# Last stage of a four-layer graph network: features in two 12-bit float32r pieces, adjacency in fp32 and bf16 pieces

## Time and profile before

| what | us |
|---|---|
| median of 3 runs | 3906.61 (3905.37 to 3919.26) |
| the profiled execution's own time | 3927.33 |
| its span, first to last instruction | 3925.3 |
| last stage in that span | 3150 to 3925.3 |
| PE busy over the span | 3393.5 (86%) |
| mean granted TensorE clock | 0.922 of 2.4 GHz |

### The profile page before, as it was taken

The page is one execution under the profiler, slowest core; times in us unless marked ns, Lnnn a source line. Parts: engine busy times, 40 slices in busy tenths (PEclk is TensorE's granted clock), DMA queues, the critical chain, the costliest instruction groups (busy, mean ns, idle before and its releaser), DMA issues. The chain is left out here.

```text
span 3925.3 us, 81257 instructions
## 1 busy us (share of the span) xinstructions
PE 3393.5 (86%) x22381; PEld 2072.9 (53%) x22381; DVE 1826.2 (47%) x5337; ACT 1453.8 (37%) x3467; POOL 1781.0 (45%) x1807
## 2 busy tenths in 40 slices
PE   4999999994875999999699989679888879999998
PEld 1566666662553555655355545345454535555554
DVE  4566666665854444453344444334444332353222
ACT  3555555552243454544233333223333331132122
POOL 1444444551015777774677777377777600000000
PEclk8988889996987999999889998789999989999999
DMA  3566666664836566665778787487777644543133
GB/s 116 170 186 192 187 184 185 178 177 80 255 116 176 157 183 176 184 178 133 201 208 223 217 229 200 118 228 208 203 205 207 164 151 171 177 153 109 55 116 123
DMA packets 717221, 675.09 MB, mean 172 GB/s; under 512 B 383123, under 2 KB 543738, under 8 KB 716810
## 3 DMA queue, kind: packets, MB, share of 16 engines
q1 hardware_dynamic: 623290, 466.05, 40.5%
q0 software_dynamic: 77008, 200.24, 18.9%
q10 hardware_dynamic: 16768, 6.91, 0.7%
HBM read 530.63 MB, written 142.28 MB: 171 GB/s over the span
## 5 line engine op out<-in xcount | busy, mean ns | idle before, releaser
L2190 POOL DMA_INDIRECT l_y<-s_lrows,l_src x1332 | 1331.9, 1000 | 456.7 <-issue 383.7
L3193 PE MATMUL ps<-nl_adj,nl_table 126*128 126x504 bf16 (+1 forms) x3150 | 631.2, 357 | 2.3 <-DVE nl_table L3428 2.3
L951 POOL DMA_INDIRECT em_gs<-s_rows,em_idx x400 | 389.6, 974 | 424.6 <-DMA em_idx<-in_sd 312.4
L3193 PEld LDWEIGHTS ps<-nl_adj,nl_table 126*128 126x128 bf16 x3150 | 301.8, 96 | 298.7 <-issue 5.0
L2230 PE MATMUL ps<-ident,l_y 128*128 128x128 f32 x1800 | 268.0, 285 | 205.7 <-DMA l_y<-s_lrows,l_src 124.1
L2273 PE MATMUL ps<-l_y,aw_pT 128*63 128x277 f32 x2700 | 384.8, 423 | 2.5 <-ACT aw_pT L2467 2.0
L2584 DVE TENSOR_TENSOR l_y<-l_y 128x768 f32<-128x768 f32 x225 | 214.0, 951 | 331.5 <-DMA l_y<-s_lrows,l_src 288.2
L2453 ACT ACTIVATE aw_yT<-ps 128x512 f32<-128x512 f32 (+1 forms) x525 | 262.0, 534 | 256.5 <-PE ps L2230 245.9
L2257 PE MATMUL ps<-aw_yT,aw_qt 128*63 128x384 f32 x1800 | 338.4, 499 | 6.9 <-DMA aw_yT<-s_dxT 6.9
L2230 PEld LDWEIGHTS ps<-ident,l_y 128*128 128x128 f32 x1800 | 205.2, 144 | 263.5 <-issue 201.8
L2619 DVE COPY aw_axd<-ps 128x252 f32<-128x252 f32 x225 | 94.6, 420 | 410.0 <-PE ps L2290 392.9
(11 more groups left out here) (375 smaller groups left out, 5872.9 us busy)
## 6 DMA issues: line engine op xcount, KB each, us to landing
nl_adj<-s_adj SPq DMA_DIRECT2D x20, 3100.8 KB
aw_yT<-s_dxT SPq DMA_DIRECT2D x150, 384.0 KB, 4.4
aw_geoS<-s_geoS SPq DMA_DIRECT2D x450, 94.5 KB
nl_adj<-s_adj SPq DMA_DIRECT2D x15, 2325.6 KB
ws_msg<-s_msg SPq DMA_DIRECT2D x75, 384.0 KB, 3.9
s_dxT<-aw_yT SPq DMA_DIRECT2D x75, 384.0 KB, 4.4
aw_qt<-s_qt SPq DMA_DIRECT2D x225, 126.0 KB
s_msg<-em_msg SPq DMA_DIRECT2D x100, 256.0 KB, 2.5
```

The source lines that it names most:

```text
L951: pool.indirect_dma_start(out=gs[:, u, j, :], out_offset=None, in_=d["rows0"], in_offset=bass.IndirectOffsetOnAxis(ap=idx[:, u, 2 * j:2 * ...
L2190: pool.indirect_dma_start(out=y[:, u, j, 0:W], out_offset=None, in_=table, in_offset=bass.IndirectOffsetOnAxis(ap=src[:, u, j:j + 1], axis ...
L3193: m = nc.tensor.matmul(k.ps[:, bank(i, p), 0:cols * WN], source[:, p, q, b, :], adj[:, a % 2, 0:cols, b * WN:(b + 1) * WN], start=b == 0 a ...
```

## The change

- The tables `table0` and `table1` hold the features as two pieces of type float32r. VectorE makes the first by clearing the low 12 bits of the fp32 word (`MASK`, a bitwise and), ScalarE copies it into the table (`HIGH`), and VectorE writes the difference as the second (`LO`). `REST` and `MID` go.
- `aggregate` has two matmuls for each source block and part, not three, both operands float32r. It goes over the adjacency in five pieces of five source blocks, both parts of `c2` within a piece.
- The adjacency stands in HBM in two banks: source blocks 0 to 14 in fp32, 15 to 24 in bf16, laid out by piece and partition. SyncE loads the three fp32 pieces of a turn straight into a ring of four buffers (`adj`). The two bf16 pieces go into a ring of three (`raw`), and POOL copies each into the ring of four, which widens it to float32r.
- `em` counts into the two banks with 315 and 210 columns (before: 273 and 273), ScalarE copies each bank for itself, and a window is stored with two DMAs.
- The positions of `make`, `turn` and `mix` in `aggregate` are other numbers, for the new order. The first adjacency load of the stage comes behind the loads of the weights, not ahead of them.
- VectorE waits, at the start of each turn, for its own last instruction of the turn before.

```diff
+PB = 5
+ADJ_BLOCKS = (15, 10)
+ADJ_TYPES = (F32, BF16)
+PIECES = tuple((bank, n) for bank in range(2) for n in range(ADJ_BLOCKS[bank] // PB))
+TOP12 = -4096
...
-                nc.scalar.activation(adj[:, v, :, h * HN:(h + 1) * HN].rearrange("p (q b) n -> p q b n", q=2),
-                                     k.ps[0:BM, ADJ:ADJ + 2, 0:KN].rearrange("p q (b n) -> p q b n", n=HN),
-                                     ACT.Copy).then_inc(adj_ok.sem, 1)
+                for q in range(2):
+                    nc.scalar.activation(adj[q][:, v, :, h * HN:(h + 1) * HN], k.ps[0:BM, ADJ + q, 0:KN[q]].rearrange("p (b n) -> p b n", n=HN),
+                                         ACT.Copy).then_inc(adj_ok.sem, 1)
...
-        table = [sb("table0", [BM, 1, 3, NB, D], BF16), sb("table1", [BM, 2, 3, NB, D], BF16)]
-        adj = sb("adj", [BM, 2, AW, NB * WN], BF16)
+        table = [sb("table0", [BM, 1, 2, NB, D], F32R), sb("table1", [BM, 2, 2, NB, D], F32R)]
+        RING, RAW = 4, 3
+        adj = sb("adj", [BM, RING, AW, PB * WN], F32R)
+        raw = sb("raw", [BM, RAW, AW, PB * WN], BF16)
...
+                for p, (bank, at) in enumerate(PIECES):
+                    g = NP_ * (i - AHEAD) + p
+                    piece = d[f"adj{bank}"][at, :, w:w + n, :]
+                    if DIRECT[p]:
+                        if g >= RING:
+                            sp.wait_ge(consumed, g - RING + 1)
+                        sp.dma_start(adj[:, g % RING, 0:n, :].bitcast(F32), piece).then_inc(adj_in[g % RING], 16)
+                    else:
+                        r = casts(g)
+                        if r >= RAW:
+                            sp.wait_ge(cast, r - RAW + 1)
+                        sp.dma_start(raw[:, r % RAW, 0:n, :], piece).then_inc(raw_in[r % RAW], 16)
...
         def _(pool):
-            nc.gpsimd.tensor_copy(idb[:, :], k.ident[:, :]).then_inc(made_id, 1)
+            nc.gpsimd.tensor_copy(idr[:, :], k.ident[0:BM, 0:BM]).then_inc(made_id, 1)
+            for i in range(AHEAD, len(turns)):
...
+                    r = casts(g)
+                    pool.wait_ge(raw_in[r % RAW], 16 * (r // RAW + 1))
+                    if g >= RING:
+                        pool.wait_ge(consumed, g - RING + 1)
+                    nc.gpsimd.tensor_copy(adj[:, g % RING, 0:n, :], raw[:, r % RAW, 0:n, :]).then_inc(cast, 1)
...
-                    for q in range(3):
+                    for q in range(2):
                         m = nc.tensor.matmul(k.ps[:, bank(i, p), 0:cols * WN], source[:, p, q, b, :],
-                                             adj[:, a % 2, 0:cols, b * WN:(b + 1) * WN],
-                                             start=b == 0 and q == 0, stop=b == NB - 1 and q == 2)
...
-                    if was != "x" and n == (8 if was == "c1" else 2):
+                    if was != "x" and at == (12 if was == "c1" else 3):
                         make(i - 1)
...
-                    nc.scalar.activation(hi, src, ACT.Copy).then_inc(s, 1)
-                    act.wait_ge(dve_.sem, dve_.of(i, "REST"))
-                    nc.scalar.activation(mid, low, ACT.Copy).then_inc(s, 1)
+                    act.wait_ge(dve_.sem, dve_.of(i, "MASK"))
+                    nc.scalar.activation(hi, top_, ACT.Copy).then_inc(s, 1)
...
-                nc.vector.tensor_tensor(low, src, hi, ALU.subtract).then_inc(s, 1)
-                dve.wait_ge(act_.sem, act_.of(i, "MID"))
-                nc.vector.tensor_tensor(lo, low, mid, ALU.subtract).then_inc(s, 1)
+                nc.vector.tensor_scalar(top_.bitcast(I32), src.bitcast(I32), TOP12, None, ALU.bitwise_and).then_inc(s, 1)
+                after("MASK")
...
+                nc.vector.tensor_tensor(lo, src, top_, ALU.subtract).then_inc(s, 1)
```

182 lines of the change are left out of this document (96 added, 86 removed).

## The result

| | before | after |
|---|---|---|
| median of 4 runs | 3905.99 us (3903.66 to 3919.26) | 3955.54 us (3944.89 to 3963.03) |
| profiled execution | 3927.3 | 3954.2 |
| em | 845.8 | 891.5 |
| last stage, to the end of the span | 768.3 | 765.6 |

The ratio is 1.0108, interval 1.0076 to 1.0140: 49 us slower by the medians, where 102 us less were forecast. The interval leaves out 1, so the loss is small but real. Of the profiled executions' difference, em has +45.7 and the last stage -2.7; aw, which the change does not touch, has -16 here and +0.6 in a second pair of traces, so that is noise. Between the two traces of the changed kernel single layers differ by more: n0 is 89.9 and 101.0 us, c1 154.9 and 142.1; differences of 10 us in one layer of one trace prove nothing where loads bind it.

What follows compares the result with a forecast made beforehand. PE's aggregate matmuls were taken to bound the kernel, except in c1; start -2, n0 -22, n1 -18, c1 +16, c2 -56, c3 -20 sum to -102 us, 3805 us at the median, range 3740 to 3870.

Steps and rivals of the forecast that it cites:

- What bounds the kernel: PE, busy 86% of the span, mostly with aggregate matmuls; 2100 for 3150 alone would give 204 us, c2 68.
- The feed: Adjacency loads: 5.08 MB a four-block turn at 357 GB/s, 14.2 us; sets n0 at 75 us against 97.1, -22.
- The start: Stretch before n0: first loads come after the weights plus some 4 us; the stretch gains only 2 us.
- The matmuls: Aggregate matmuls in float32r take 0.2175 us with 504 columns and 0.163 with 378, as in bf16.
- The upper term that I kept for the range: Weight loads under 378-column matmuls: up to 0.05 us might stand out, on 900 matmuls at most 45 us.
- slower than a column a cycle: Rival, every aggregate matmul: float32r at two columns' time, about 4085 us; decides from 0.33 us a matmul; chance 0.09.
- The casts: POOL's two casts a turn, 2.3 us each, hold VectorE's two-operand steps: +4.6 us a four-block turn in c1.
- c1 in the whole change: Layer c1 with casts and slow make: 23.5 us a four-block turn, 18.4 three-block; 147.5 us against 131.5, +16.
- The row chain of c1: ScalarE and VectorE steps from one TAKE to the next in c1: 17.3 us a four-block turn without casts.
- em: Stage em: ScalarE's two copies add 25 us on an idle engine, PE loses 4; taken as 0, ends -4 and +8.
- The range: Whole kernel: 3740 to 3870 us, from the free casts to the slow end of the feed; slow matmul outside.
- The rival that ended slower: Rival in the aggregate matmuls: float32r streams slower than a column a cycle, about 4085 us; chance 0.09.

Runs made afterwards that it cites:

- best: Kernel before with two bf16 feature pieces and the change's aggregate order, MASK, HIGH and LO; old whole-turn loads: ratio 0.9705 and 0.9692 to before.
- bf2: Changed kernel with feature pieces and adjacency all in bf16, no casts: last stage 605.0 us, ratio 0.9701 to the kernel before.
- f_feed: bf2 with the changed kernel's fp32 and bf16 adjacency transfers put back, no casts, bf16 matmuls: last stage 747.2 us.
- serial1: Changed kernel, but each adjacency load is issued only when the one before has landed: last stage 929.8 us.
- order: Changed kernel, but each turn's bf16 pieces are issued before the fp32 ones and the first adjacency loads before the weights: ratio 0.9981 to the kernel before.
- f_casts: bf2 with two raw pieces a turn and POOL's casts put back, bf16 matmuls, no larger load: last stage 661.3 us.
- f_pitch: bf2 with float32r matmuls put back, on a tile that stays in SBUF, no cast or larger load: last stage 630.7 us.

## Why the prediction was wrong, point by point

- **What bounds the kernel** was right for before: with two bf16 pieces for three, and so a third fewer matmuls, the last stage falls by 144 (best) or 154 us (bf2), c2 by 64, of the 68 that the matmuls alone were to give. Both runs also have the shorter row chain (no MID); no run removes the matmuls alone.
- **The feed** is the step that failed. I took 357 GB/s for five loads of 0.64 to 1.27 MB from the earlier trace rows, which is one load of 3.18 MB alone, and expected larger packets to help if anything; the slow end was 320. Measured: 230 in f_feed, 246 to 281 in the changed kernel's n0 and n1, a four-block turn of 16.6 to 23.6 us instead of 14.2. In the changed kernel the engines stand for 17 or 18% of the time, about which my term had nothing, and are slower by 5 to 16% while they work; in f_feed they stand little and are slower by a quarter. It missed n0 by 15 us, n1 by 35, c3 by 17.
- **The start** is an error of its own. "Some 4 us" was to be the first load's time from its issue. Its packets stand behind those of the weights' loads for about 5 us of the 12.84, and a lone load fares no better (12.1 in serial1). The stretch got 11.5 us longer instead of 2 shorter; with the load ahead of the weights n0 starts 7.6 us sooner (order). The load is not all of it: bf2, with the same order and smaller loads, has 49.2 us, and the casts alone add 4.9 to that.
- **The matmuls**: 0.2175 taken, 0.2416 measured. The upper term that I kept for the range (a fixed 0.05 on 378 columns) had the wrong form; it is a rate. It accounts for c2: 400 matmuls by 0.0241 and 300 by 0.0188 are 15.3 us, and c2 missed by 12. The rival "slower than a column a cycle" was right in kind, but at 11% far below the 0.33 us from which it was to decide alone. The Trainium skill, "FP8 and Floating Point Precision", TensorE Precision Notes, only says that the reduced mode reads 4 bytes and truncates, and that true fp32 takes four passes. The trace agrees that a float32r matmul is not at the price of fp32: 0.2416 us, where the forecast worked out 0.85 for fp32.
- **The casts** were right in kind: 2.3 us each alone (2.29 in the trace), and VectorE's two-operand steps held. In size they were too dear: in the turn of c1 shown two casts held two steps for 2.9 us, not 4.6. That c1 is 143.7 in f_casts where I had 147.5, with a four-block turn of 22.05 for 23.5, comes of two errors against each other, this one and a chain that was put too short (the point after next). The casts cost the last stage 56 us when alone. That one operand in SBUF is free, as I had it, holds for the steps that read PSUM (0.69 beside a cast) and not for MASK (2.15 instead of 0.43).
- **c1 in the whole change** came out at 154.9 against 147.5 (142.1 in the second trace), and that it is so near is luck. Its first two turns, which wait for loads, took 24.0 and 34.7 us where I had 14.2 and 26, and its four-block turns after them 21.1 to 21.8 where I had 23.5, the three-block ones 16.6 and 15.2 where I had 18.4. No row stood behind the 26.
- **The row chain of c1** without casts was to be 17.3 us a turn: 17.4 in f_pitch with PE at 2.4 GHz, 19.1 in bf2 with make at 1.2. I had counted the slow make only together with the casts.
- **em** was put at 0, with ends -4 and +8, from ScalarE's copy and PE's columns alone: 25 us more of copies expected, 20.8 measured, and ScalarE as a whole was busy for only 4.3 us more. The place of the cost was not on my list at all: 413 KB stored a window instead of 258, counted alike (630 packets of 840 or 420 bytes, and 126 of 2100 before). em cost 34 to 46 us more, and without that the change would have been about even with before.
- **The range** failed because each bound of the feed came from rows with one load in flight, and because em had no bound of its own size. The rival that ended slower named another mechanism. Of the 151 us between forecast and median, em has 34 to 46 and the last stage 100: the start 14, n0 15, n1 35, c1 7, c2 12, c3 17. What decided was a bandwidth term too high by a quarter to a half, plus a stage that I had costed by its instructions and not by its bytes.

## What to carry to other kernels

A rate read while one large load streams is not the rate of the same volume cut in five: ask also for how long the engines will stand between the pieces, and before cutting one load into five, find a row in which several are in flight, or measure one. For the first load of a stage, count what is already queued ahead of it. When operands get wider, cost every stage that writes or reads them in bytes, also those that the change "only" stores from. And put the parts of a change back one at a time on the fastest common base: it showed in three runs that the saving in matmuls was real (150 us) and that the fp32 adjacency alone can eat nearly all of it.
